# Group convolution on one Trainium2 core: from twelve accumulating products per step to four 32-column tiles fed from rows gathered through DRAM

## The chip, the cores and the metric

One core of a Trainium2 chip runs the whole program. The number reported is the time of one execution on the device in microseconds (us); lower is better. Three executions were timed (median 732.78 us, from 731.9 to 734.84), and one more was profiled.

## What is computed

The input `x` is 128 samples of 32 rows by 512 columns. In short, for each sample:

```
a  = mixing(x, cond)                  # 32x32 row mix per sample, weights from a small network on cond
x1 = x + attention(a) @ Wo            # 32 query heads of 16, 8 key/value heads, causal over the 32 rows
z  = conv1d(x1, weight)               # 9 taps along the 512 columns, pad 4; 4 groups of 8 channels in, 8 out
     + cond @ c_weight.T + bias       #   (a channel is one of the 32 rows)
out = x1 + z @ base_W.T + base_b + lora(z)   # lora: 8 experts of rank 16, weighted by a router
router: softmax(z @ router_W.T + router_b) over 15, the 8 largest kept
```

Products that need full precision use a split of each float32 value into a high and a low part (three matmuls: high*high, high*low, low*high); the convolution, the mixing and the transposes use plain float32.

## The kernel before, in words

**Tiling.** Four samples (128 rows) form a group; there are 32 groups. The 512 columns are kept as 4 phases of 128 (column 4n+j is phase j, index n). The work of a group is spread over four steps of a software pipeline: `iterate` calls every engine's `steps(t)` for t from -1 to 34, of which t = 4 to 30 run as a hardware loop and the rest are written out. In step t the engines do the queries, keys, scores, softmax and values of group t, the mixing of group t+1, the output projection (`project`) and the convolution of group t-1, the feed-forward product of group t-2 and the last (lora) part of group t-3.

**Order.** Each engine has its own list, written out by hand, and waits on semaphores. There is no scheduler. TensorE in step t (lines 605 to 652): `queries`, `keys_values`, `lora`, `project`, `transpose_qk`, `mix`, `scores`, `feed_forward`, `transpose_p`, `values`, `conv`, `transpose_hw`, `transpose_o`. A helper `product` (line 377) issues the split matmuls of `queries`, `keys_values` and `project`.

**The convolution** (lines 552 to 560): for each of 4 samples and each of 3 shifts one float32 matmul, 128 x 128 into 128 columns, with the input itself as the stationary operand. So the input must lie with (phase, channel) on the partitions. `by_phase` (line 280) makes that layout, `x1ph`, out of `x1` with 16 copies of 32 x 128: 8 on ScalarE (its copies are recorded at line 665) and 8 on VectorE (line 284). Output rows come out as the pixels, so that `zs` (after the addition at line 1031 of `convb`, a bias that was broadcast to 2 MB in the prologue) is split into `z_hi` (ScalarE) and `z_lo` (GpSimd, line 808) and used as stationary operand of `feed_forward` straight away.

**feed_forward** (lines 524 to 534): 12 terms, each one matmul into bank 6 (384 columns) and one into bank 7 (272 columns: the last phase of the base product, and the lora and router columns), in turn. `ar_ps` is raised at the end. ScalarE then copies `arS`; VectorE does `route`, ScalarE `ex`, VectorE `route2`, which ends with `hw` (line 971); TensorE needs that in `transpose_hw` (line 585), before `transpose_o` (line 591), which itself needs `normalize` (lines 1018, 1020).

**SyncE's queue** in a step (lines 346 to 357): load `xr` once `x1` is written, store `out` once it is there, load the next `xm` once `mix` is done.

**Prologue.** Tap weights are transposed and masked to `convW`; `ctxb` and `convb` are built; in step 0 TensorE waits for the loaded mixing weights (`mixw_in2`) and mixes before `scores(0)`, and runs 8 extra products after `prepare_ar` (`keep_warm`, line 430).

## Time and profile before

| what | value |
|---|---|
| timed executions, median (lowest to highest) | 732.78 us (731.9 to 734.84) |
| profiled execution, its own time | 736.14 us |
| its span in the profile | 733.8 us |
| TensorE matmul busy | 696.9 us, 95% of the span |
| VectorE busy | 528.8 us, 72% |
| ScalarE busy | 262.8 us, 36% |
| GpSimd busy | 149.5 us, 20% |
| instructions | 13835 |
| DMA | 35.45 MB, 48 GB/s over the span |
| mean granted TensorE clock | 0.99 |

The span runs from the first to the last instruction; the execution's own time has 2.3 us more around it. A float32 matmul is recorded as two loads and two matmuls, so the 12 matmuls of the convolution stand as 24. Durations of matmuls overlap by pipelining; the distance from one start to the next is what a matmul costs in a stream. A line "engine line op out<-in xN" merges N instructions in a row.

### The profile page before, as it was taken

The numbers are of one execution on the slowest core, as the hardware profiler recorded it, in microseconds if no ns is written. First come the engines' busy times: TensorE is split into PE (matmuls) and PEld (weight loads), VectorE is DVE, ScalarE is ACT, GpSimd is POOL, SyncE is SP. The second block draws the span as 40 slices with busy tenths as digits, with TensorE's granted clock in tenths as the row PEclk, the third lists the DMA queues.
The fourth block names the chain that finished last, engine by engine and source line by source line (L and its number), as shares of the span: only waits on it lengthen the run. The fifth ranks groups of instructions, "written<-read, shape, count | busy, mean of one in ns | idle before, by whom it ended". The sixth has DMA issues, their size and how long they took to land.

```text
span 733.8 us, 13835 instructions
## 1 busy us (share of the span) xinstructions
PE 696.9 (95%) x4850; PEld 623.2 (85%) x4882; DVE 528.8 (72%) x1488; ACT 262.8 (36%) x635; POOL 149.5 (20%) x116
## 2 busy tenths in 40 slices
PE   6799999999999999999999999999999999999994
PEld 4578989888988988898888888988888898888884
DVE  5557777777777777777787777777777777777763
ACT  4244443432344343333433332344333234433330
POOL 6222111122112121221212122121212212121211
PEclk9999999999999999999999999999999999999997
DMA  7870011110011111100111110011111001110100
GB/s 175 167 269 29 30 44 44 43 43 24 21 41 43 43 43 43 34 23 29 43 43 43 43 43 14 29 43 43 43 43 43 14 29 43 43 43 29 29 15 29
DMA packets 27394, 35.45 MB, mean 48 GB/s; under 512 B 11651, under 2 KB 13347, under 8 KB 26998
## 3 DMA queue, kind: packets, MB, share of 16 engines
q1 hardware_dynamic: 26374, 34.87, 16.0%
q0 software_dynamic: 144, 0.28, 0.2%
q10 hardware_dynamic: 864, 0.14, 0.1%
q8 instruction: 7, 0.11, 0.1%
q14 instruction: 5, 0.04, 0.0%
HBM read 26.35 MB, written 8.93 MB: 48 GB/s over the span
## 4 chain that ended last, share of the span: by engine, by line
PE 89%; ACT 3%; SPq 3%; issue 2%; DVE 2%; DMA 1%; DVEq 0%
PE ps L377 31%; PE ps L558 12%; PE ps L532 10%; PE ps L577 8%; PE ps L533 6%; PE ps L547 5%; PE ps L473 4%; PE ps L507 3%; ACT raw L665 3%; PE ps L565 2%; PE ps L591 2%; PE ps L521 2%; PE ps L543 2%; SPq L308 1%; DMA mixw_dram<-convb 1%
## 5 line engine op out<-in xcount | busy, mean ns | idle before, releaser
L665 ACT ACTIVATE qk_t<-ps 128x512 f32<-128x512 f32 x32 | 19.1, 597 | 226.8 <-PE ps L522 226.8
L822 POOL TENSOR_TENSOR y_lo<-ys,y_hi 128x512 fp32r<-128x512 f32 x31 | 39.4, 1271 | 267.4 <-ACT y_hi L665 267.4
L665 ACT ACTIVATE x1ph<-raw 32x128 f32<-32x128 f32 x256 | 79.0, 309 | 40.8 <-DVE raw L1063 38.2
L558 PE MATMUL ps<-convW,x1ph 128*128 128x128 f32 x768 | 92.6, 277 | 0.4 <-ACT x1ph L665 0.4
L377 PE MATMUL ps<-wqkv_hi,y_hi 128*128 128x512 f32 (+1 forms) x256 | 90.8, 355 | 0.4
L558 PEld LDWEIGHTS ps<-convW,x1ph 128*128 128x128 f32 x768 | 88.3, 192 | 0.7 <-ACT x1ph L665 0.7
L377 PE MATMUL ps<-wqkv_hi,y_lo 128*128 128x512 f32 (+1 forms) x256 | 87.5, 342 | 0.0
L377 PE MATMUL ps<-wqkv_lo,y_hi 128*128 128x512 f32 (+1 forms) x256 | 87.5, 342 | 0.0
L816 POOL TENSOR_TENSOR raw<-raw,basebB 128x512 f32<-128x512 f32 x32 | 49.3, 1540 | 143.5 <-DVE raw L1055 143.5
L577 PEld LDWEIGHTS ps<-vm,raw 128*128 128x128 f32 x512 | 59.6, 191 | 15.9 <-ACT raw L665 13.2
L577 PE MATMUL ps<-vm,raw 128*128 128x68 f32 x512 | 63.9, 278 | 8.4 <-ACT raw L665 8.4
L808 POOL TENSOR_TENSOR z_lo<-raw,z_hi 128x512 fp32r<-128x512 f32 x32 | 41.2, 1288 | 145.7 <-ACT z_hi L665 145.7
L981 DVE TENSOR_TENSOR network<-ps,cst 128x512 f32<-128x512 f32 x64 | 31.5, 491 | 53.2 <-PE ps L377 51.8
L1009 DVE TENSOR_REDUCE mx<-ps 128x16 f32<-128x512 f32 x64 | 43.9, 686 | 31.3 <-PE ps L547 31.3
L377 PEld LDWEIGHTS ps<-wqkv_hi,y_hi 128*128 128x128 f32 x256 | 48.9, 191 | 12.5 <-issue 5.6
L284 DVE COPY x1ph<-raw 32x128 f32<-32x128 f32 x256 | 55.7, 217 | 3.0
L377 PEld LDWEIGHTS ps<-wqkv_lo,y_hi 128*128 128x128 f32 x256 | 49.1, 192 | 6.1
L377 PEld LDWEIGHTS ps<-wqkv_hi,y_lo 128*128 128x128 f32 x256 | 48.9, 191 | 6.0
L377 PE MATMUL ps<-wo_hi,oT_hi 128*128 128x512 f32 x128 | 51.7, 404 | 0.0
L377 PE MATMUL ps<-wo_lo,oT_hi 128*128 128x512 f32 x128 | 50.3, 393 | 0.0
L377 PE MATMUL ps<-wo_hi,oT_lo 128*128 128x512 f32 x128 | 50.3, 393 | 0.0
L1000 DVE TENSOR_TENSOR qk_t<-ps,cst 128x512 f32<-128x512 f32 x32 | 22.1, 691 | 36.9 <-PE ps L522 36.9
(176 smaller groups left out, 1523.0 us busy)
## 6 DMA issues: line engine op xcount, KB each, us to landing
xm<-x SPq DMA_DIRECT2D x32, 256.0 KB, 2.6
xr<-x SPq DMA_DIRECT2D x32, 256.0 KB, 2.8
out<-raw SPq DMA_DIRECT2D x32, 256.0 KB, 2.0
convb<-convb_dram SPq DMA_DIRECT2D x1, 2048.0 KB, 11.6
mixb<-mixb_dram SPq DMA_DIRECT2D x1, 1792.0 KB, 7.3
raw<-L_attn_Wq SPq DMA_DIRECT2D x4, 256.0 KB, 5.5
raw<-L_attn_Wo SPq DMA_DIRECT2D x8, 128.0 KB, 5.1
raw<-L_ffn_base_W SPq DMA_DIRECT2D x1, 1024.0 KB, 5.9
```

The source lines that it names most:

```text
L284: last = copy(x1ph[S * j:S * (j + 1), b, 1:P + 1], x1[S * b:S * (b + 1), j, :])
L377: last = mm(dst, a, b, start=(n == 0), stop=(n == 3 * len(left) - 1))
L532: mm(ps[:, 6, 0:BASE6], a[:, j, :], b[:, j, 0:BASE6], start=first, stop=False)
L533: last = mm(ps[:, 7, 0:P + NAR], a[:, j, :], b[:, j, BASE6:D + NAR], start=first, stop=final)
L547: last = mm(ps[:, h, b * P:(b + 1) * P], qT[rows, b, :, :].rearrange("p g q -> p (g q)"), kT[rows, b, :, :].rearrange("p k m -> p (k m)"), ...
L558: last = mm(zo[:, :, b * S:(b + 1) * S], x1ph[:, b, s:s + P], convW[:, s, :, :], start=(s == 0), stop=(s == SHIFTS - 1))
L577: last = mm(ps[:, 4 + k // 4, (k % 4) * NB * VW:(k % 4 + 1) * NB * VW], prT[:, k, :], vm[:, k, :, :].rearrange("p b c -> p (b c)"), start= ...
L665: return nc.scalar.activation(dst, src, ACT.Copy)
L808: nc.gpsimd.tensor_tensor(z_lo[:, :, :].rearrange("p j n -> p (j n)"), zs, z_hi[:, :, :].rearrange("p j n -> p (j n)").bitcast(F32), ALU.s ...
L816: nc.gpsimd.tensor_tensor(x1b, x1, basebB[:, :].rearrange("p (n j) -> p j n", j=PH), ALU.add).then_inc(x1b_sb, 1)
L822: nc.gpsimd.tensor_tensor(y_lo[:, :], ys[:, :], y_hi[:, :].bitcast(F32), ALU.subtract).then_inc(y_lo_sb, 1)
L1009: v.tensor_reduce(m, s3, AX.X, ALU.max).then_inc(mx_sb, 1)
```

## The change

Input to the convolution: `x1` now has a column of zeros on either side of each phase. It is stored to DRAM (`x1_dram`) in each step, then gathered back with three DMAs, one per shift, into `xc`: 96 partitions (shift, 8 channels of a group, 4 phases) by 16 (sample, group) by 128. Each group of channels is one float32 matmul, 96 rows, 32 stationary columns, 512 moving columns, whose result goes to partitions 32g to 32g+31 of bank 1. The tap weights are the stationary operand now. The result has (channel, phase) on the partitions; the bias is per partition (`biasT`), and four transposes turn it back (`transpose_z`, after `transpose_qk` of the next step) into bank 7, from which `z_hi` and `z_lo` are made; `z_lo` goes from GpSimd to VectorE. `feed_forward` issues the 12 matmuls into bank 7 first, then the 12 into bank 6. `transpose_hw` goes ahead of `conv`. On VectorE the `x1` addition goes ahead of `keys`, `route` behind `softmax`, `route2` ahead of `normalize`. GpSimd makes `x1c` (x1 plus bias) and copies it to `x1b` in the next step. The prologue loses `ctxb`, `convb` and its 2 MB load, and the 8 extra products of step 0; there `mix(1)` and its wait come after `scores(0)` and `prepare_conv`.

```diff
...
     for t in range(G - 1, G + 3):
         steps(t)
-def by_phase(copy, phases):
-
-    for j in phases:
-        for b in range(NB):
-            last = copy(x1ph[S * j:S * (j + 1), b, 1:P + 1], x1[S * b:S * (b + 1), j, :])
-    return last
+def z_transposed():
+
+    return ps[:, 7, :].rearrange("p (q j o) -> p j q o", j=PH, o=CG)
 block = ctx.enter_context(nc.Block())
...
 load_mixw(1, 4, mixw_in2)
 sp.dma_start(rawbase, baseW.rearrange("(p j) l -> p j l", j=PH)).then_inc(ld["base"], 16)
 sp.dma_start(mixw_dram[4 * NB:B, :, :], aggS[4 * NB:B, :, :]).then_inc(mixw_out, 16)
-sp.wait_ge(ctx_sb, 1)
-sp.dma_start(convb_dram, ctxb[:, :]).then_inc(ctx_dram, 16)
 sp.wait_ge(mixw_out, 16)
 load_mixw(4, G, mixw_in)
 sp.dma_start(mixb[:, 4 * P:], mixb_row[4 * P:].partition_broadcast(P)).then_inc(mixb_in2, 16)
-sp.wait_ge(ctx_dram, 16)
-sp.wait_ge(mixw0_sb, 1)
-sp.wait_ge(mixb0_ps, 1)
-sp.dma_start(convb[:, :], convb_dram.rearrange("b s -> (b s)").partition_broadcast(P)).then_inc(convb_in, 16)
 def steps(t):
-    if live(t - 1):
-        wait(sp, x1_sb, t - 1)
-        sp.dma_start(xr[:, :], group(x_g, t - 1)).then_inc(xr_in, 16)
     if live(t - 3):
         wait(sp, out_sb, t - 2)
         sp.dma_start(group(out_g, t - 3), outS).then_inc(out_st, 16)
+    if live(t - 1):
+        sp.wait_ge(x1_sb, t)
+        sp.dma_start(x1_dram.rearrange("q (i j) n -> (q i) j n", j=PH), x1p[:, :, :]).then_inc(x1_out, 16)
     if live(t + 1) and live(t + 2) and not peeled(t, -1):
         wait(sp, y_ps, t + 2)
         sp.dma_start(xm[:, :], group(x_g, t + 2)).then_inc(xm_in, 16)
+
+    if live(t):
+
+        wait(sp, z_ps, t - 1)
+        sp.dma_start(xr[:, :], group(x_g, t)).then_inc(xr_in, 16)
+    if live(t - 1):
+        if not live(t):
+            wait(sp, z_ps, t - 1)
+        sp.wait_ge(x1_out, 16 * t)
+        for s in range(SHIFTS):
+            sp.dma_start(xc[S * s:S * (s + 1), :, :],
+                         x1_dram[:, :, s:s + P].rearrange("q r n -> r q n")).then_inc(xc_in, 16)
 for t in range(-1, 4):
     steps(t)
...
         if j % 2:
             last.then_inc(arT_ps, 1)
+def prepare_conv():
+
+    pe.wait_ge(cvR_sb, 1)
+    for j in range(PH):
+        nc.tensor.transpose(ps[0:SHIFTS * S, 4, j * S:(j + 1) * S],
+                            cvR[:, j, :, :, :].rearrange("o s i a -> o (s i a)"),
+                            cst[0:S, C_ID:C_ID + S])
+    pe.wait_ge(fsideR_sb, 1)
+    pe.wait_ge(ones_sb, 1)
+    mm(ps[:, 4, P:P + B], ccT[:, :, :, :].rearrange("p g j o -> p (g j o)"), condT[:, :], start=True, stop=False)
+    mm(ps[:, 4, P:P + B], fsideR[:, :, :, :].rearrange("p g j o -> p (g j o)"), ones8[0:1, :], start=False, stop=True
+       ).then_inc(cv_ps, 1)
+
 def prepare_lora():
     pe.wait_ge(ld["B"], 16 * PH)
...
     pe.wait_ge(z_hi_sb, u + 1)
     pe.wait_ge(z_lo_sb, u + 1)
     wait(pe, out_sb, u)
-    for j in range(PH):
-        for n, (a, b) in enumerate(((z_hi, ffn_hi), (z_hi, ffn_lo), (z_lo, ffn_hi))):
-            first, final = j == 0 and n == 0, j == PH - 1 and n == 2
-            mm(ps[:, 6, 0:BASE6], a[:, j, :], b[:, j, 0:BASE6], start=first, stop=False)
-            last = mm(ps[:, 7, 0:P + NAR], a[:, j, :], b[:, j, BASE6:D + NAR], start=first, stop=final)
+    terms = [(a[:, j, :], b[:, j, :]) for j in range(PH)
+             for a, b in ((z_hi, ffn_hi), (z_hi, ffn_lo), (z_lo, ffn_hi))]
+    for n, (a, b) in enumerate(terms):
+        last = mm(ps[:, 7, 0:P + NAR], a, b[:, BASE6:D + NAR], start=(n == 0), stop=(n == len(terms) - 1))
     last.then_inc(ar_ps, 1)
+    for n, (a, b) in enumerate(terms):
+        mm(ps[:, 6, 0:BASE6], a, b[:, 0:BASE6], start=(n == 0), stop=False)
 def scores(t):
     pe.wait_ge(qT_sb, t + 1)
...
                 last.then_inc(s_ps, 1)
 def conv(u):
-    pe.wait_ge(ph_act, u + 1)
-    pe.wait_ge(ph_dve, u + 1)
-    zo = ps[:, 1, :].rearrange("p (j t) -> p j t", j=PH)
+    pe.wait_ge(xc_in, 16 * SHIFTS * (u + 1))
+    for g in range(S // CG):
+        last = mm(ps[S * g:S * (g + 1), 1, :], convW[:, g, :, :].rearrange("p j o -> p (j o)"),
+                  xc.rearrange("p (b g) n -> p g b n", g=S // CG)[:, g, :, :],
+                  start=True, stop=True)
+    last.then_inc(z_ps, 1)
+
+def transpose_z(u):
+    pe.wait_ge(zs_sb, u + 1)
     for b in range(NB):
-        for s in range(SHIFTS):
-            last = mm(zo[:, :, b * S:(b + 1) * S], x1ph[:, b, s:s + P],
-                      convW[:, s, :, :], start=(s == 0), stop=(s == SHIFTS - 1))
-    last.then_inc(z_ps, 1)
+        last = nc.tensor.transpose(ps[:, 7, b * P:(b + 1) * P], zs[:, b * P:(b + 1) * P], ident)
+    last.then_inc(zT_ps, 1)
 def transpose_p(t):
     pe.wait_ge(p_sb, 2 * (t + 1))
...
 if live(t):
     transpose_qk(t)
+if live(t - 2):
+    transpose_z(t - 2)
 if peeled(t, 1):
     pe.wait_ge(prep_sb, 1)
     prepare_base((0, 1))
 if peeled(t, -1):
     pe.wait_ge(mixw0_sb, 1)
-if peeled(t, 0):
-    pe.wait_ge(mixw_in2, 16 * NB)
 if peeled(t, 2):
     pe.wait_ge(mixw_in, 16 * NB)
-if live(t + 1):
+if live(t + 1) and not peeled(t, 0):
     mix(t + 1)
 if peeled(t, -1):
     mixing_weights()
...
 if peeled(t, 0):
     prepare_ar()
-    pe.wait_ge(cv_sb, 1)
-    keep_warm(8)
+    prepare_conv()
+    pe.wait_ge(mixw_in2, 16 * NB)
+    mix(t + 1)
 if peeled(t, 1):
     prepare_base((2, 3))
     pe.wait_ge(x1_sb, 1)
...
 if live(t):
     transpose_p(t)
+if peeled(t, 0):
+    pe.wait_ge(convW_sb, 1)
 if live(t):
     values(t)
+if live(t - 2):
+    transpose_hw(t - 2)
 if live(t - 1):
     conv(t - 1)
-if live(t - 2):
-    transpose_hw(t - 2)
 if live(t):
     transpose_o(t)
...
 if live(t):
     act.wait_ge(qT_ps, t + 1)
     copy(qT, ps[:, 2, :].rearrange("p (g b q) -> p b g q", g=NQ, b=NB)).then_inc(qT_sb, 1)
+if live(t - 2):
+    act.wait_ge(zT_ps, t - 1)
+    copy(z_hi[:, :, :].rearrange("p j (q o) -> p j q o", o=CG), z_transposed()).then_inc(z_hi_sb, 1)
 if peeled(t, 1):
     prepare_base((0, 1))
-if live(t - 1):
-    act.wait_ge(x1_sb, t)
-    by_phase(copy, (1, 3)).then_inc(ph_act, 1)
-if live(t):
-    for h in range(2):
+for h in range(2):
+    if live(t):
         act.wait_ge(sx_sb, 2 * t + 1 + h)
         nc.scalar.activation(pr.rearrange("p (h k b m) -> p h b k m", h=2, k=HK, b=NB)[:, h, :, :, :],
                              sx.rearrange("p (h b k m) -> p h b k m", h=2, b=NB, k=HK)[:, h, :, :, :],
                              ACT.Exp, scale=HD ** -0.5).then_inc(p_sb, 1)
+    if h == 0 and live(t - 2):
+        act.wait_ge(ar_ps, t - 1)
+        copy(arS[:, :], ps[:, 7, P:P + NAR]).then_inc(ar_sb, 1)
+if live(t - 2):
+    act.wait_ge(lgs_sb, t - 1)
+    nc.scalar.activation(ex[:, :], lgs[:, :], ACT.Exp).then_inc(ex_sb, 1)
+if live(t):
     for h in range(2):
         act.wait_ge(pT_ps, 2 * t + 1 + h)
         copy(prT[:, 4 * h:4 * h + 4, :].rearrange("p k n -> p (k n)"), ps[:, 2 + h, :]).then_inc(pT_sb, 1)
-if live(t - 2):
-    act.wait_ge(ar_ps, t - 1)
-    copy(arS[:, :], ps[:, 7, P:P + NAR]).then_inc(ar_sb, 1)
 if live(t + 1):
     act.wait_ge(ys_sb, t + 2)
     copy(y_hi[:, :], ys[:, :]).then_inc(y_hi_sb, 1)
...
 def steps(t):
     if live(t - 2):
-        pool.wait_ge(zs_sb, t - 1)
-        pool.wait_ge(z_hi_sb, t - 1)
-        nc.gpsimd.tensor_tensor(z_lo[:, :, :].rearrange("p j n -> p (j n)"), zs,
-                                z_hi[:, :, :].rearrange("p j n -> p (j n)").bitcast(F32),
-                                ALU.subtract).then_inc(z_lo_sb, 1)
-    if live(t - 2):
-        pool.wait_ge(x1_sb, t - 1)
+
+        wait(pool, out_sb, t - 2)
+        pool.wait_ge(x1c_sb, t - 1)
+        if peeled(t, 2):
+            pool.wait_ge(pads_sb, 1)
+        nc.gpsimd.tensor_tensor(x1b, x1c, zero[:, :].unsqueeze(2).broadcast_to([P, PH, P]), ALU.add).then_inc(x1b_sb, 1)
+    if live(t - 1):
+        pool.wait_ge(x1_sb, t)
         pool.wait_ge(ld["basebB"], 16)
-
-        wait(pool, out_sb, t - 2)
-        nc.gpsimd.tensor_tensor(x1b, x1, basebB[:, :].rearrange("p (n j) -> p j n", j=PH),
-                                ALU.add).then_inc(x1b_sb, 1)
+        wait(pool, x1b_sb, t - 1)
+        nc.gpsimd.tensor_tensor(x1c, x1, basebB[:, :].rearrange("p (n j) -> p j n", j=PH),
+                                ALU.add).then_inc(x1c_sb, 1)
     if peeled(t, 0):
         prepare_wo((0, 1))
     if live(t + 1) and not peeled(t, -1):
...
 def steps(t):
     if peeled(t, 2):
-        dve.wait_ge(convb_in, 16)
         dve.wait_ge(baseT_ps, PH)
     if live(t - 2):
         dve.wait_ge(z_ps, t - 1)
-        v.tensor_tensor(zs.rearrange("p (j n) -> p j n", j=PH), ps[:, 1, :].rearrange("p (j n) -> p j n", j=PH),
-                        convb[:, bass.ds((t - 2) * P, P)].unsqueeze(1).broadcast_to([P, PH, P]),
+        v.tensor_tensor(zs.rearrange("p (b n) -> p b n", b=NB), ps[:, 1, :].rearrange("p (b n) -> p b n", b=NB),
+                        biasT[:, bass.ds((t - 2) * NB, NB)].unsqueeze(2).broadcast_to([P, NB, P]),
                         ALU.add).then_inc(zs_sb, 1)
     if live(t - 3):
         dve.wait_ge(hwT_hi_sb, t - 2)
...
     out3 = outS.rearrange("p (n j) -> p j n", j=PH)
     v.tensor_tensor(out3[:, 0:3, :], ps[:, 6, 0:BASE6].rearrange("p (j n) -> p j n", j=3), x1b[:, 0:3, :], ALU.add)
     v.tensor_tensor(out3[:, 3, :], ps[:, 5, 0:P], x1b[:, 3, :], ALU.add).then_inc(out_sb, 1)
-if live(t):
-    keys(t)
 if live(t - 1):
     dve.wait_ge(wo_ps, t)
     dve.wait_ge(xr_in, 16 * t)
-    wait(dve, x1b_sb, t - 1)
+    wait(dve, x1c_sb, t - 1)
+    wait(dve, x1_out, 16 * (t - 1))
     v.tensor_tensor(x1, ps[:, 4, :].rearrange("p (j n) -> p j n", j=PH),
                     xr[:, :].rearrange("p (n j) -> p j n", j=PH), ALU.add).then_inc(x1_sb, 1)
+if live(t):
+    keys(t)
+if live(t - 2):
+    dve.wait_ge(z_hi_sb, t - 1)
+    minus(z_lo[:, :, :].rearrange("p j (q o) -> p j q o", o=CG), z_transposed(),
+          z_hi[:, :, :].rearrange("p j (q o) -> p j q o", o=CG)).then_inc(z_lo_sb, 1)
 if peeled(t, 1):
     prepare_base((0, 1))
 if live(t):
     softmax(t)
+if live(t - 2):
+    route(t - 2)
 if peeled(t, -1):
     prepare_q(0)
     dve.wait_ge(mixb0_sb, 1)
...
```

## Rows read from the trace of the kernel before

**Rows 1.** The profile's page: TensorE's busy time; the chain by engine, by line.
```profile
PE 696.9 (95%) x4850; PEld 623.2 (85%) x4882; DVE 528.8 (72%) x1488; ACT 262.8 (36%) x635; POOL 149.5 (20%) x116
...
PE 89%; ACT 3%; SPq 3%; issue 2%; DVE 2%; DMA 1%; DVEq 0%
PE ps L377 31%; PE ps L558 12%; PE ps L532 10%; PE ps L577 8%; PE ps L533 6%; PE ps L547 5%; PE ps L473 4%; PE ps L507 3%; ACT raw L665 3%; PE ps L565 2%; PE ps L591 2%; PE ps L521 2%; PE ps L543 2%; SPq L308 1%; DMA mixw_dram<-convb 1%
```
**Rows 2.** Busy time by engine in one stretch; then clock, DMA share, GB/s.
```profile
319.00:340.30 21.30, 20.90 (x151) 18.88 (x151) 15.94 (x46) 7.73 (x19) 4.10 (x3) 1.00 0.10 37
```
**Rows 3.** The chain in order of time: queries of steps 4 and 31.
```profile
108.00 4.17 PE ps L377 x24
...
683.16 4.17 PE ps L377 x24
```
**Rows 4.** The page's costliest groups: the convolution and what feeds it.
```profile
L665 ACT ACTIVATE x1ph<-raw 32x128 f32<-32x128 f32 x256 | 79.0, 309 | 40.8 <-DVE raw L1063 38.2
L558 PE MATMUL ps<-convW,x1ph 128*128 128x128 f32 x768 | 92.6, 277 | 0.4 <-ACT x1ph L665 0.4
...
L284 DVE COPY x1ph<-raw 32x128 f32<-32x128 f32 x256 | 55.7, 217 | 3.0
```
**Rows 5.** TensorE in one step of the loop, in order of time.
```profile
330.59 0.38 PE L543 MATMUL ps<-causal,ident 128*128 128x512 bf16 x1
330.90 1.16 PE L547 MATMUL ps<-qk_t 64*128 64x128 f32 x16
331.99 0.44 PE L532 MATMUL ps<-ffn_hi,z_hi 128*128 128x384 f32 x1
...
335.69 1.04 PE L565 MATMUL ps<-cst,raw 128*128 128x128 f32 x8
336.98 2.00 PE L577 MATMUL ps<-vm,raw 128*128 128x68 f32 x16 [0.25 <-ACT raw L665]
338.82 2.89 PE L558 MATMUL ps<-convW,x1ph 128*128 128x128 f32 x24
341.55 0.28 PE L585 MATMUL ps<-cst,hw 128*128 128x128 f32 x1
341.67 0.60 PE L591 MATMUL ps<-cst,raw 128*128 128x128 f32 x4
```
**Rows 6.** TensorE in the prologue, in order of time.
```profile
14.10 2.08 PE L473 MATMUL ps<-mixw,xm 128*128 128x128 f32 x8
16.11 3.78 PE L424 MATMUL ps<-convb,attT 8*128 8x512 f32 x4
```
**Rows 7.** VectorE in the same step as rows 5.
```profile
330.19 1.05 DVE L1063 TENSOR_TENSOR raw<-ps,xr 128x512 f32<-128x512 f32 x1
332.09 0.69 DVE L1009 TENSOR_REDUCE mx<-ps 128x16 f32<-128x512 f32 x1 [0.85 <-PE ps L547]
...
339.31 0.42 DVE L1020 TENSOR_TENSOR raw<-ps,rz 128x256 f32<-128x256 f32 x1
```
**Rows 8.** DMA issues: KB each, median us from issue to landing.
```profile
xr<-x SPq DMA_DIRECT2D x32, 256.0 KB, 2.8
out<-raw SPq DMA_DIRECT2D x32, 256.0 KB, 2.0
...
raw<-L_attn_Wv SPq DMA_DIRECT2D x1, 256.0 KB, 7.0
```
**Rows 9.** Busy time by engine while the weights load; last number GB/s.
```profile
10.00:15.00 5.00, 3.23 (x15) 2.45 (x15) 3.51 (x12) 2.79 (x8) 3.22 (x6) 1.00 1.16 257
```
**Rows 10.** Waits: TensorE's `mix(1)`, for the mixing weights.
```profile
PE ps L473 <- DMA mixw<-mixw_dram: 2.2, 1, 2.2
```
**Rows 11.** The last steps: TensorE and ScalarE, in order of time.
```profile
712.91 2.94 PE L558 MATMUL ps<-convW,x1ph 128*128 128x128 f32 x24 [0.44 <-ACT x1ph L665]
...
724.81 0.29 ACT L665 ACTIVATE arS<-ps 128x144 f32<-128x144 f32 x1 [7.56 <-PE ps L533]
...
727.93 0.33 PE L585 MATMUL ps<-cst,hw 128*128 128x128 f32 x1 [3.16 <-DVE hw L971]
```

126 lines of the change are left out of this document (56 added, 70 removed).

## The prediction, made before the changed kernel was run

> **What bounds the kernel now.** I read the busy times first: TensorE is at it for 696.9 of 733.8 us, and the chain that ended last is 89% TensorE, of which line 558, the convolution, is 12% [rows 1]. Then one stretch in the middle: of 21.30 us TensorE works 20.90 at the full clock, VectorE 15.94, ScalarE 7.73, GpSimd 4.10, and the DMA engines are a tenth used [rows 2]. Then the chain in order of time: the queries of step 4 start at 108.00 and those of step 31 at 683.16, so a step takes 575.16 / 27 = 21.30 us [rows 3]. So the loop is TensorE's list, played without gaps (the only one of note is 0.25 us ahead of the values [rows 5]). What shortens that list counts 32 times; what is taken off ScalarE or VectorE counts only if TensorE waits for it.
>
> **The convolution now.** Its 24 records stand from 338.82 to the next one at 341.55: 2.73 us, 0.114 each [rows 5]. All 768 take 92.6 us by their busy time [rows 4]. Taken away: 2.73 per step. With it go the 16 layout copies: 79.0 us on ScalarE and 55.7 on VectorE over the run [rows 4], 2.5 and 1.7 a step. Both engines have idle time, so I cost that at nothing; its worth is slack.
>
> **The four tiles.** Each new matmul streams 512 columns where an old one streams 128. What does a plain float32 record of 512 columns take? The prologue has four, at half the pace: 3.78 / 4 = 0.95, right behind 128-column ones of 2.08 / 8 = 0.26 [rows 6]; a quarter of the one is 0.24, so time goes with columns, and at full pace a record is 4 x 0.114 = 0.455. There are 8 of them (two per matmul). In series that is 3.64, worse than now. If the four tiles run side by side it is two slots, 0.91. Those are the two ends. The nearest row is the scores' (line 547), which use 64 rows of the array each: 16 records begin at 330.90 and feed_forward follows at 331.99, 1.09 for what would be 1.82 in series and 0.91 in 8 slots of two [rows 5]. So parts of the array do work side by side, with 0.18 around them. I take full overlap and 0.2 for going in and out: 1.11 per step.
>
> The Trainium skill, TensorE: Matmul & The Clock Gate, Part 3, says that weight loads overlap with running matmuls only where their row groups differ, and here all four tiles use the same rows. By that rule the loads would stand in the open. No row here shows a 32-column load; as an estimate, a quarter of a 128-column record is 0.03, eight of them 0.23 per step, and the forecast would be 7 us higher. It lies inside my range, and I don't take it, since the same part measures column tiles as nearly as quick as row tiles.
>
> **Transposing back.** Four more transposes; the eight of line 565 take 1.04 with their tail, and four of line 591 0.60 where each start is 0.11 from the last [rows 5]: 0.45 per step. The two orders of feed_forward hold the same 24 matmuls, 3.70 us from 331.99 to 335.69: nothing.
>
> Sum per step: -2.73 + 1.11 + 0.45 = -1.17, and 32 groups: -37.4.
>
> **What could now be late, step by step** (times of the step in rows 5 and 7, all moved 0.45 later by the transposes where TensorE sets them).
> *The scores* need kT. The x1 addition came behind keys and ended at 331.24 [rows 7]; with the two swapped, kT is there at 331.24 if nothing starts sooner, and x1 at 330.55 (keys is a pass of the size of line 1009's, 0.69 [rows 7]). The scores' first product would start at 330.59 + 0.45 = 331.04 [rows 5]: at most 0.2 lost.
> *z_lo* is one more such pass on VectorE, till 331.9 (z_hi, on ScalarE, runs beside keys); feed_forward starts at 332.44 [rows 5]. Covered by 0.5.
> *The probabilities*: softmax [rows 7] starts 0.45 later, like feed_forward's end; the arS copy of 0.3 [rows 11] goes between the two exponentials, which are two VectorE passes apart. Nothing.
> *The router chain*: from the arS copy to hw's transpose it is 727.93 - 724.81 = 3.1 us when nothing is in its way [rows 11]. Bank 7 is now done halfway, near 334.2, but VectorE takes it up after softmax (332.54 and four passes of 0.69: 335.3) and puts ys in between: 335.3 + 3.1 - 0.3 + 0.7 = 338.8, and transpose_hw comes at 341.55 - 2.73 + 0.45 = 339.3 [rows 5]. Covered by 0.5.
> *transpose_o* waits for normalize, whose last multiply ended at 339.73, 0.91 after the convolution had started [rows 5, 7]. Before, 2.73 us of convolution covered that; now transpose_hw (0.11) and 1.11. Cover by 0.3, and less if route2, now ahead of normalize on VectorE, is late: from 339.0 two halves of some 0.65 end at 340.3, and transpose_o is due at 340.5. The thinnest place; each 0.1 lost there costs 3.2 us.
> *SyncE's queue*: out, then the x1 store, xm (behind mix), xr, then it waits for the x1 store and issues three gathers. Behind that wait stands only the next step's out store. *GpSimd* does 3 passes as before, 4.1 us of 20.
>
> **The round trip.** x1 is written by 330.6. The out store of the same size lands in 2.0, a load in 2.8 [rows 8]; the x1 rows come in smaller pieces, so landed 2.4 to 3.2 later: 333.0 to 333.8. The gathers move 3 x 256 KB; in the prologue, with pieces of 512 bytes and less among them, 257 GB/s were moved [rows 9]: 3.1 us, and some 1.5 of latency (2.8 less what 256 KB take at that rate): 337.6 to 338.4. The convolution would want it at 339.4. So it is hidden, with 1.0 to 1.8 us to spare. The other end is a load of 512-byte pieces that landed in 7.0 us in a crowded queue [rows 8].
>
> **Prologue and end.** Step 0 waited 2.2 us for the mixing weights with the scores behind it [rows 10]; now the scores cover that; the 8 extra products go, about as much conv preparation comes, and values(0) waits for convW. I take -1.5 (0 to -4). At the end conv(31) began 0.44 after its layout copies [rows 11]; now a store and gathers, 2.4 + 4.6 = 7 us by the figures above, stand in a stretch with 3.7 us of feed_forward: about +3. Against it the router chain of the last group, 3.1, runs beside the base columns. I take 0 (-2 to +4).
>
> **Sum.** -37.4 - 1.5 + 0 = -38.9, plus 0.1 per step for small new waits (an estimate from the two places with 0.2 to 0.3 of cover), 3: -36. The profiled execution took 736.14, so it would be 700; it stood 3.4 above the median of the timed ones, and against 732.78 it is **697 us**.
>
> **Rivals.**
> *A, the tiles overlap only in part.* The Trainium skill, same page and part, says that matmuls start and end strictly in program order. A float32 matmul is two records on one tile, so the second of tile 0 must wait for its first, and tile 1 behind it. As a mechanism of this kernel: slots 0a | 0b 1a | 1b 2a | 2b 3a | 3b, five of 0.455 = 2.28, and the step is -2.73 + 2.48 + 0.45 = +0.20: +6.4 - 1.5, **738**. The scores' 1.09 us would fit 9 such slots (1.02) about as well as 8 (0.91), so the trace doesn't exclude it; for the forecast speaks that it needs 0.18 of switching in the one case and 0.07 in the other, and switching of almost nothing is less likely. Chance 0.10.
> *B, no overlap at all*: 3.64 + 0.2, +1.56 a step, **781**. Rows 5 speak against it for row tiles; column tiles aren't in the trace. 0.06.
> *C, slower by the gathers.* Place: TensorE's wait ahead of conv. If a gather takes the 7.0 us of rows 8 from its issue (333.4, and an estimated 0.8 for the two issues ahead), it lands at 341.2, 1.8 late each step: -36 + 58, **755**. It decides from 5.2 us of landing on; above 6.4 the kernel is slower than before. For it: 1536 small pieces, xm and xr in the same queue. Against it: the DMA engines are a tenth busy [rows 2], and the 7.0 was queued behind six other loads. 0.10, half of it light.
> *D, it does less than it says*: the convolution shrinks, but TensorE then waits for normalize or kT, half a microsecond each step: **713**. 0.06.
> Forecast: 0.68.
>
> **Chances and range.** A measurement of this kernel tells 0.5%, 3.7 us, from no change. Faster: 0.68 + D 0.06 + light C 0.03 = 0.77. Same: parts of A and C, 0.05. Slower: 0.18. The forecast's own range is 684 (no new waits, prologue -4) to 710 (loads in the open, small waits doubled); to leave out no more than 2 in 10 it reaches over D and light C to 732.
>
> **What would show it.** Right: a step of 20.1 to 20.3 us; eight conv records in about 1.1 us, starting in fours; waits ahead of conv for the gather near zero; conv's chain share about 5%; ScalarE and VectorE down by some 70 and 35 us. Wrong: conv records 0.45 apart (B) or starting in pairs (A); TensorE waiting on a DMA into xc, or a landing time over 5 us (C); an idle ahead of line-591 transposes on normalize, or ahead of the scores (D).

## The result, and the profile after

The changed kernel takes **709.45 us** (median of 4 executions, 704.92 to 711.31), the kernel before beside it 733.22 (4 executions, 731.9 to 734.84): ratio 0.965, 95% interval 0.962 to 0.968, a gain of 24 us where 36 were forecast. The profiled executions are 709.07 and 736.14 us, 27.1 apart; the one of before stood about 3 above its median, the one of after at its own. The gain is clear of the spread; its size is two thirds of the forecast.

The profile's page of the changed kernel: busy times, the chain that ended last, and the time from issue to landing of the DMAs (the last number, in us). `scratch<-x_dram` are the gathers into `xc`.

```profile
PE 660.4 (93%) x4455; PEld 557.2 (79%) x4487; DVE 499.2 (71%) x1264; ACT 181.0 (26%) x379; POOL 141.3 (20%) x117
...
PE 86%; DMA 5%; ACT 3%; issue 3%; DVE 2%; SPq 1%; DVEq 0%; ACTq 0%
PE ps L381 33%; PE ps L543 9%; PE ps L590 8%; PE ps L540 7%; PE ps L564 5%; PE ps L556 4%; PE ps L481 4%; DMA scratch<-x_dram 4%; PE ps L515 3%; PE ps L604 3%; ACT raw L681 2%; PE ps L578 2%; PE ps L529 2%; PE ps L572 2%; PE ps L552 2%
...
scratch<-x_dram SPq DMA_DIRECT2D x96, 256.0 KB, 5.2
x_dram<-x1p SPq DMA_DIRECT2D x32, 260.0 KB, 2.0
xm<-x SPq DMA_DIRECT2D x32, 256.0 KB, 2.8
xr<-x SPq DMA_DIRECT2D x32, 256.0 KB, 2.9
```

Against [rows 1], TensorE has 36.5 us less work, the convolution fell from 12% of the chain to 5% (line 564), and ScalarE lost 82 us, VectorE 30. New in the chain is a DMA at 4%, of which more below. One step of the loop, as in [rows 2]:

```profile
299.00:319.30 20.30, 19.63 (x143) 16.77 (x142) 15.14 (x38) 5.14 (x11) 3.83 (x3) 1.00 0.35 90
```

The chain in order of time has the queries of the steps as in [rows 3]; the first and the last of 25 steps without a wait in them:

```profile
145.88 4.20 PE ps L381 x24
...
653.29 4.20 PE ps L381 x24
```

(653.29 - 145.88) / 25 = 20.30 us each, against 21.30; the 27 from step 4 to step 31 average 20.31. DMA share went from 0.10 to 0.35. TensorE in the stretch that changed, beside [rows 5]:

```profile
357.09 0.60 PE L572 MATMUL ps<-cst,raw 128*128 128x128 f32 x4
357.53 1.06 PE L481 MATMUL ps<-mixw,xm 128*128 x8
359.00 0.38 PE L552 MATMUL ps<-causal,ident 128*128 128x512 bf16 x1 [0.42 <-issue]
359.31 1.16 PE L556 MATMUL ps<-qk_t 64*128 64x128 f32 x16
...
367.27 0.28 PE L598 MATMUL ps<-cst,hw 128*128 128x128 f32 x1
367.48 1.07 PE L564 MATMUL ps<-scratch,convW 96*32 96x512 f32 x8
368.47 0.66 PE L604 MATMUL ps<-cst,raw 128*128 128x128 f32 x4
```

By starts, the convolution takes 368.47 - 367.48 = 0.99 us (2.73 before), `transpose_hw` ahead of it 0.21 (0.12 before), the transposes back 0.44, and 0.42 us of idle stand ahead of the scores. In the kernel before that idle was 0.15:

```profile
373.25 0.38 PE L543 MATMUL ps<-causal,ident 128*128 128x512 bf16 x1 [0.15 <-issue]
```

That is -2.73 + 0.99 + 0.09 + 0.44 + 0.27 = -0.94 of the measured -0.99. The rest lies in the stretches around it, as means over 25 steps: from `transpose_o` to the next queries 0.54 before and 0.40 after, against some 0.07 more in the projections and `feed_forward`.

**Where the 27 us came from** (spans 733.8 and 706.8; starts of the queries of each step):

| stretch | before | after | difference | forecast |
|---|---|---|---|---|
| to the start of step 1 | 43.4 | 41.3 | -2.1 | -1.5 |
| steps 1 to 3 | 64.4 | 63.3 | -1.1 | -3.2 |
| steps 4 to 30, 27 of them | 575.2 | 548.5 | -26.7 | -28.9 |
| queries of step 31 to the end | 50.8 | 53.7 | +2.9 | -2.1 |

(The forecast's column splits its -1.07 a step over the convolutions in each stretch: 3, 27 and 2.) The loop did nearly what was said; the edges kept the rest. But only the loop repeats: of the kernels below, e11 has the changed kernel's steps 1 to 3 and its end, and took 61.5 and 52.4 us for them where this execution took 63.3 and 53.7. So some 3 us of the edges are this execution's and not the kernel's.

### The profile page after: what moved, and what is told of

Same layout as the page of the kernel before. It is cut to its first block, busy times and chain, and to the rows that moved or that the text cites. A ratio compares the mean times of both kernels' runs of the same rounds, so it can differ in the third digit from the quotient of the medians.

```text
span 706.8 us, 12716 instructions
## 1 busy us (share of the span) xinstructions
PE 660.4 (93%) x4455; PEld 557.2 (79%) x4487; DVE 499.2 (71%) x1264; ACT 181.0 (26%) x379; POOL 141.3 (20%) x117
## 4 chain that ended last, share of the span: by engine, by line
PE 86%; DMA 5%; ACT 3%; issue 3%; DVE 2%; SPq 1%; DVEq 0%; ACTq 0%
PE ps L381 33%; PE ps L543 9%; PE ps L590 8%; PE ps L540 7%; PE ps L564 5%; PE ps L556 4%; PE ps L481 4%; DMA scratch<-x_dram 4%; PE ps L515 3%; PE ps L604 3%; ACT raw L681 2%; PE ps L578 2%; PE ps L529 2%; PE ps L572 2%; PE ps L552 2%
## 5 line engine op out<-in xcount | busy, mean ns | idle before, releaser
L826 POOL TENSOR_TENSOR raw<-raw,zero 128x512 f32<-128x512 f32 x32 | 33.2, 1038 | 281.0 <-DVE raw L1073 281.0
L681 ACT ACTIVATE qk_t<-ps 128x512 f32<-128x512 f32 x32 | 19.1, 597 | 238.8 <-PE ps L530 238.8
L756 ACT ACTIVATE raw<-raw 128x512 f32<-128x512 f32 x64 | 40.5, 632 | 130.1 <-DVE raw L1030 130.1
L831 POOL TENSOR_TENSOR raw<-x1p,basebB 128x512 f32<-128x512 f32 x32 | 49.0, 1531 | 47.4 <-DVE x1p L1080 47.4
L1080 DVE TENSOR_TENSOR x1p<-ps,xr 128x512 f32<-128x512 f32 x32 | 35.2, 1099 | 29.7 <-PE ps L381 29.7
L1030 DVE TENSOR_TENSOR raw<-ps,mx 128x512 f32<-128x512 f32 x64 | 44.3, 692 | 2.2
L543 PE MATMUL ps<-ffn_hi,z_lo 128*128 128x384 f32 x128 | 43.9, 343 | 0.0
L543 PE MATMUL ps<-ffn_lo,z_hi 128*128 128x384 f32 x128 | 43.8, 342 | 0.0
```

The costliest lines, as they stand in the source:

```text
L543: mm(ps[:, 6, 0:BASE6], a, b[:, 0:BASE6], start=(n == 0), stop=False)
L681: return nc.scalar.activation(dst, src, ACT.Copy)
L756: nc.scalar.activation(pr.rearrange("p (h k b m) -> p h b k m", h=2, k=HK, b=NB)[:, h, :, :, :], sx.rearrange("p (h b k m) -> p h b k m", ...
L831: nc.gpsimd.tensor_tensor(x1c, x1, basebB[:, :].rearrange("p (n j) -> p j n", j=PH), ALU.add).then_inc(x1c_sb, 1)
L1030: v.tensor_tensor(sx[:, D * h:D * h + D].rearrange("p (h m) -> p h m", m=S), s3, m.unsqueeze(2).broadcast_to([P, 16, S]), ALU.subtract).th ...
L1080: v.tensor_tensor(x1, ps[:, 4, :].rearrange("p (j n) -> p j n", j=PH), xr[:, :].rearrange("p (n j) -> p j n", j=PH), ALU.add).then_inc(x1_ ...
```

## The experiments

Twelve kernels, each the changed kernel with one edit unless said otherwise; e10 and e12 were executed six and five times, the others once. A step is the mean from the queries of step 4 to those of step 31; it repeats within 0.02 us from one execution to the next (20.31, and 20.30 in four kernels that didn't change it). The total doesn't (last section), nor do the edges, so the step is what I compare.

### Is it the overlap of the four tiles?

**e1**: all four products write to partitions 0 to 31.

```diff
-    last = mm(ps[S * g:S * (g + 1), 1, :], convW[:, g, :, :].rearrange("p j o -> p (j o)"),
+    last = mm(ps[0:S, 1, :], convW[:, g, :, :].rearrange("p j o -> p (j o)"),
...
```

> The changed kernel with all four matmuls of the convolution sent to the same 32 columns of the array (partitions 0 to 31), one after another, so three quarters of z are stale; the same loads, streams, DMAs and order otherwise. Theory (the gain of the convolution is that four tiles run side by side): eight records 0.455 us apart, 3.64 instead of 0.91, 2.7 us more per step: a step of 23.0 us, some 795 us in all. Rival (the gain comes from fewer and longer instructions, or from the copies taken off ScalarE and VectorE, and the tiles matter little): below 720 us.

Measured: 786.0 us, step 22.86, +2.54.

```profile
357.36 3.62 PE L564 MATMUL ps<-scratch,convW 96*32 96x512 f32 x8
360.91 0.66 PE L604 MATMUL ps<-cst,raw 128*128 128x128 f32 x4
```

3.55 us from start to next start against 0.99: rival B's price nearly to the figure (3.64), and the whole gain is the overlap, 3.6 times. In the changed kernel's trace the first four matmul records of the convolution start within 0.02 us of each other and the other four 0.45 us later. The records don't say which tile they belong to, but on one tile, in e1, each starts 0.43 to 0.45 after the last, so four that start together must be on four tiles. Two slots of four: rival A, five slots, isn't what happens.

### Do the transposes back cost their 0.45?

**e2**: one of the four.

```diff
-    for b in range(NB):
+    for b in range(1):
         last = nc.tensor.transpose(ps[:, 7, b * P:(b + 1) * P], zs[:, b * P:(b + 1) * P], ident)
```

> The changed kernel with one of the four transposes of z instead of four; the rest of z is stale. Theory (the loop is TensorE's list played without gaps): three transposes of 0.11 less, a step of 19.97 instead of 20.30, 10 us less in all. Rival (a gather from DRAM ends last ahead of the convolution, with 0.4 us to spare or none): the step shrinks by 0.1 or less, since the x1 addition, the store and the gathers start from the projection, which stands ahead of the transposes.

Measured: 709.85 us, step 20.30, unchanged. Three transposes fewer, and the idle ahead of the scores grew from 0.42 to 0.74, by what they took:

```profile
359.87 0.27 PE L572 MATMUL ps<-cst,raw 128*128 128x128 f32 x1
...
361.77 0.38 PE L552 MATMUL ps<-causal,ident 128*128 128x512 bf16 x1 [0.74 <-issue]
```

The theory "TensorE's list has no gap here" falls. The scores' start is set elsewhere; VectorE at the same time in the changed kernel shows by what:

```profile
356.99 1.09 DVE L1080 TENSOR_TENSOR x1p<-ps,xr 128x512 f32<-128x512 f32 x1 [0.93 <-PE ps L381]
358.01 0.68 DVE L1019 TENSOR_TENSOR qk_t<-ps,cst 128x512 f32<-128x512 f32 x1
```

The keys (line 1019) come behind the `x1` addition and end at 358.69, and the scores begin 0.31 later. That distance is 0.32 us in every one of 25 steps, in this kernel, in e2 and in the kernel before alike. The timeline calls the idle "issue", but in step 0, where TensorE waits longer, the same distance stands between the two (29.14 to 29.45), and there it names the keys (`qk_t`); e7 tests it:

```profile
29.45 0.38 PE L552 MATMUL ps<-causal,ident 128*128 128x512 bf16 x1 [1.05 <-DVE qk_t L1019]
```

### Did the layout copies matter?

**e3**: the kernel *before*, with 2 of its 16 copies (1 on each engine).

```diff
-            for j in phases:
-                for b in range(NB):
+            for j in phases[:1]:
+                for b in range(samples):
```

(`samples` is 1.)

> The kernel before with 2 of its 16 layout copies (one on ScalarE, one on VectorE), so the convolution reads stale input; TensorE's list is unchanged. Theory (copies on ScalarE and VectorE were hidden behind TensorE and their removal is worth nothing in the loop): a step of 21.2 to 21.3 us as before, at most 3 us less in all (the last convolution no longer waits 0.44 us). Rival (part of the gain of the change comes from relieving ScalarE and VectorE): 10 us or more less.

Measured: 732.93 us beside 734.69, step 21.29 beside 21.30. Taking away 14 copies, some 120 us of engine time over the run, is worth nothing by itself, as costed.

### Is "router columns first" needed?

**e4**: `feed_forward` in the order of before, bank 6 and bank 7 in turn, all else as changed.

```diff
     for n, (a, b) in enumerate(terms):
+        mm(ps[:, 6, 0:BASE6], a, b[:, 0:BASE6], start=(n == 0), stop=False)
         last = mm(ps[:, 7, 0:P + NAR], a, b[:, BASE6:D + NAR], start=(n == 0), stop=(n == len(terms) - 1))
     last.then_inc(ar_ps, 1)
-    for n, (a, b) in enumerate(terms):
-        mm(ps[:, 6, 0:BASE6], a, b[:, 0:BASE6], start=(n == 0), stop=False)
```

> The changed kernel with feed_forward's 24 matmuls in the order of the kernel before (bank 6 and bank 7 in turn), so that the router columns are complete 1.9 us later. Theory (the halves are issued apart because ScalarE and VectorE now have route and the arS copy ahead of work that TensorE waits for): ScalarE stands at arS while the second exponential is ready, the transposes of the probabilities start 0.5 to 1.3 us late, and normalize is late behind route2: a step of 20.9 to 21.9 us instead of 20.30, 20 to 45 us more in all. Rival (the order is only for the last group, where the chain of the router stands alone): a step of 20.30 and 2 to 3 us more at the end.

Measured: 743.0 us beside 732.77, step 21.37, +1.06. ScalarE in one step and TensorE in the one before, in order of time (lines 681, 756 and 578 of the changed kernel stand one higher here):

```profile
377.25 0.29 ACT L680 ACTIVATE arS<-ps 128x144 f32<-128x144 f32 x1 [1.71 <-PE ps L541]
```

```profile
356.74 1.09 PE L577 MATMUL ps<-cst,raw 128*128 128x128 f32 x8 [0.90 <-ACT raw L755]
```

ScalarE holds the second exponential back behind the `arS` copy, which waits for the last of `feed_forward`; the probabilities come 0.9 us late. So "router columns first" is no extra. Without it, and with the engines' other new orders as they are, the whole gain is lost: the step is that of the kernel before (21.37 against 21.30), and of the 10 us above it 8 are the end (58.6 us from the queries of step 31 on, against 50.8).

### The gathers: hidden in the loop, bare at the end

**e5**: one gather instead of three in all steps but the first; it waits for that one.

```diff
-    for s in range(SHIFTS):
+    for s in range(SHIFTS if peeled(t, 1) else 1):
...
-    pe.wait_ge(xc_in, 16 * SHIFTS * (u + 1))
+    pe.wait_ge(xc_in, 16 * (u + SHIFTS))
```

> The changed kernel with one gather of three from the second group on (two thirds of the gathered rows are stale from the first group). Theory (the gathers are hidden in the loop and exposed at both ends): a step of 20.30 us as before, the wait ahead of the last convolution (2.5 us) shrinks to about 1 and the clock falls for less long at the end: 2 to 6 us less in all. Rival (the gather is what ends last in every step): a step shorter by 0.1 us or more.

Measured: 704.62 us, step 20.30, unchanged; the end from step 31 on 49.6 us against 53.7. In the loop, then, the gathers cost nothing. SyncE in the changed kernel:

```profile
317.52 0.34 SPq L346 DMA_DIRECT2D x_dram<-x1p  x1
318.24 0.34 SPq L349 DMA_DIRECT2D xm<-x  x1
318.84 0.34 SPq L354 DMA_DIRECT2D xr<-x  x1
319.58 1.39 SPq L360 DMA_DIRECT2D scratch<-x_dram  x3
```

and its waits on the gathers (in all, times, the longest):

```profile
PEld ps L564 <- DMA scratch<-x_dram: 4.4, 4, 2.7
```

Four waits in 32 steps, all near the two ends. But the margin is thin. In the step of these rows the last of the three gathers lands at 326.01 and the convolution starts at 326.88. Over 25 steps the rows are there 0.3 to 1.1 us ahead of it, 0.5 at the median. (The page's 5.2 us is the median of all 96 gathers; the third of each step takes 5.3 to 6.1 us, 5.9 at the median.)

**e6**: gathers issued ahead of `xm` and `xr` on SyncE. The queue's wait on the last convolution (`z_ps`) goes, since the wait on `x1` behind that convolution implies it.

> The changed kernel with the three gathers ahead of the loads of xm and xr in SyncE's queue, without the wait on the last convolution that the order of the others implies. Theory (gathers hidden in the loop, competing with 512 KB of other loads): they land about 1 us sooner, the step stays at 20.30 us because nothing waits for them. Rival (the 0.1 us ahead of the convolution is a wait for the gather): step 20.2.

Measured: 705.5 us, step 20.30. The page:

```profile
scratch<-x_dram SPq DMA_DIRECT2D x96, 256.0 KB, 4.3
...
xm<-x SPq DMA_DIRECT2D x32, 256.0 KB, 4.9
xr<-x SPq DMA_DIRECT2D x32, 256.0 KB, 5.0
```

The gathers land 0.9 us sooner by their median, the two loads behind them 2.1 later, and neither moves the step: nothing in the loop waits for either. The rows are now there 1.0 to 1.5 us ahead of the convolution.

**e7**: on VectorE, `keys` ahead of the `x1` addition again. **e8**: this and e6's order together.

```diff
+    if live(t):
+        keys(t)
     if live(t - 1):
         dve.wait_ge(wo_ps, t)
...
-    if live(t):
-        keys(t)
```

> The changed kernel with keys ahead of the x1 addition on VectorE, as before the change. Theory (what holds TensorE in the loop is kT, late by 0.3 us at the scores, which is why leaving out three transposes gained nothing): the idle ahead of the scores falls from 0.42 to about 0.1, but x1 is 0.7 later and with it store and gathers, which have 0.4 us to spare: 0.3 gained at the scores less 0.6 lost ahead of the convolution, a step of 20.4 to 20.7 us. Rival (the gathers have more to spare than 0.4): a step of 20.0.

> Keys ahead of the x1 addition, and the gathers ahead of xm and xr. Theory: both waits are gone, a step of 20.0 us, some 8 us less in all than the changed kernel. Rival (store and gathers from the later x1 still end last): 20.2 or more, with a DMA wait ahead of the convolution.

Measured: e7 717.55 us, step 20.69, slower; e8 694.83 us, step 19.98. In e7 the idle ahead of the scores is gone, as the reading of e2 has it, but another has come:

```profile
363.74 1.06 PE L481 MATMUL ps<-mixw,xm 128*128 x8
364.85 0.38 PE L552 MATMUL ps<-causal,ident 128*128 128x512 bf16 x1
...
373.11 0.28 PE L598 MATMUL ps<-cst,hw 128*128 128x128 f32 x1
373.81 1.06 PE L564 MATMUL ps<-scratch,convW 96*32 96x512 f32 x8 [0.42 <-DMA scratch<-x_dram]
```

```profile
PEld ps L564 <- DMA scratch<-x_dram: 26.8, 31, 2.3
```

Counted from the step's first query, `x1` is written 0.9 us later and the whole round trip with it, while the scores and all behind them come 0.4 sooner. A margin of 0.5 can't pay for both, and nearly every step waits now, 0.2 to 1.1 us each, 0.6 on average. In e8 the sooner landing pays. TensorE in e8:

```profile
369.41 1.06 PE L477 MATMUL ps<-mixw,xm 128*128 x8
370.51 0.38 PE L548 MATMUL ps<-causal,ident 128*128 128x512 bf16 x1
```

No idle ahead of the scores, and none ahead of the convolution in this part of the loop either (its eight records begin at 359.05, 0.21 behind `transpose_hw`). But it is just in time: the last gather lands at 359.01. Over the whole run e8's weight loads wait for a gather in 13 steps:

```profile
PEld ps L560 <- DMA scratch<-x_dram: 6.1, 13, 2.2
```

Within the loop TensorE loses at most 0.2 us by it in a step, so the gather is the next bound, with nothing to spare. So the changed kernel's two orders (the addition first, the loads first) are each one half of a pair: turned back alone the one is neutral and the other a loss, both together are worth 0.32 us a step, 9 over the loop. e8's total, 15 under the changed kernel's, has a quick start in it (last section). And e7 is rival C in small: the gather does become the bound once it starts 0.9 later.

### The end

The changed kernel's last steps: TensorE in order of time, and a window of the last 23 us:

```profile
687.65 1.94 PE L564 MATMUL ps<-scratch,convW 96*32 96x512 f32 x8 [2.51 <-DMA scratch<-x_dram]
...
694.83 0.57 PE L540 MATMUL ps<-ffn_hi,z_hi 128*128 128x272 f32 x1 [1.46 <-DVE z_lo L850]
```

```profile
684.00:707.00 23.00, 12.54 (x50) 9.64 (x50) 7.30 (x25) 1.66 (x5) 1.04 (x1) 0.70 0.16 44
```

2.5 us for the gather, and behind it a convolution of 1.94 instead of 1.07 and `feed_forward` at 0.23 from one start to the next instead of 0.125: the granted clock of this stretch (the last number but two of the window's row) is 0.70, so much of it ran at 1.2 GHz, not 2.4. **e9**: 10 products whose result nobody reads, ahead of the last convolution, in the time in which TensorE waits for the gather.

```diff
+    if peeled(t, G):
+        pe.wait_ge(x1_sb, G)
+        keep_warm(10)
     if live(t - 1):
         conv(t - 1)
```

> The changed kernel with ten extra 512-column bf16 products into a free bank in step 32, between transpose_hw and the last convolution, where TensorE waits 2.5 us for the gather. Theory (the end of the changed kernel lost 3 to 4 us because TensorE stood still there and then worked at 1.2 GHz: the last convolution took 1.94 instead of 1.07 and feed_forward's first 19 matmuls twice their time): the clock stays up after the wait, from the queries of step 31 to the end 53.7 us become 49 to 51. Rival (the end is set by the chain of transfers and copies, not by the clock): 53 or more.

Measured: 708.99 us; from step 31 to the end 49.95 instead of 53.73.

```profile
688.91 2.11 PE L425 MATMUL ps<-causal,ident 128*128 128x512 bf16 x9
690.95 1.06 PE L564 MATMUL ps<-scratch,convW 96*32 96x512 f32 x8
```

```profile
684.00:707.00 23.00, 13.60 (x82) 10.18 (x82) 8.83 (x34) 2.16 (x7) 1.48 (x2) 0.94 0.24 65
```

The clock of the same stretch is 0.94, the convolution back at 1.06, and the end 3.8 us shorter. Not all of that is the clock: here the last convolution starts 34.2 us behind the queries of step 31, 0.4 sooner than in the changed kernel's execution. And e11, whose end is the changed kernel's too, needed 52.4 us. From the start of the last convolution on it is 15.75 us here, 19.1 in the changed kernel and 18.5 in e11, so the products are worth some 3 us. The total hides it: step 1 of this execution started at 46.4, 5 us later than in the changed kernel's (41.3).

### The start

**e11**: `mix(1)` ahead of `scores(0)`, as before the change.

```diff
+    if peeled(t, 0):
+        pe.wait_ge(mixw_in2, 16 * NB)
-    if live(t + 1) and not peeled(t, 0):
+    if live(t + 1):
         mix(t + 1)
...
-    pe.wait_ge(mixw_in2, 16 * NB)
-    mix(t + 1)
```

> The changed kernel with mix(1) and its wait for the mixing weights ahead of scores(0) again, as before the change. Theory (the order of step 0 is worth the wait of 2.2 us that it hides): the queries of step 1 start at 43 to 44 us instead of 40 to 41.5, the loop as it was (20.30). Rival (the start of step 1 is set by the chain of normalize and projection weights, or by the clock): 40 to 42.

Measured: 707.27 us, step 1 at 43.0, the lower edge of what the theory gives. Inconclusive: kernels with one and the same step 0 started step 1 anywhere from 40.1 to 46.4.

### All together

**e10**: e8 and e9 in one.

> Keys ahead of the x1 addition, gathers ahead of xm and xr, and the ten extra products of the last step, together. Theory: the parts add up: a step of 19.98 as in the kernel with the first two, an end 3 us shorter: 691 to 693 us, a ratio to the kernel before of 0.942 to 0.947. Rival (the one look at the first two was a lucky prologue): 697 or more, 0.950 or more.

Measured: median **697.03 us** (6 executions, 694.48 to 701.36) against 735.65 of the kernel before (11 executions, 732.73 to 739.55): ratio 0.947, interval 0.944 to 0.950, against 0.965 (0.962 to 0.968) of the change: some 12 us faster than the changed kernel. The ratio is at the theory's upper edge; the median is not the theory's 691 to 693 but where the rival begins, and with executions from 694.5 to 701.4 these runs don't tell the two apart. The step is 20.02, so the loop's part is there. The end took 51.1 us in the profiled execution, not e9's 50.0, and 1.8 less than e8's where 3 were said. Its last convolution ran at full pace, but the `feed_forward` behind it fell back to half pace, 0.23 us from one start to the next for its first 12 matmuls.

**e12**: e10 with ten more such products in step 0, 6 behind the keys and values and 4 behind `transpose_qk`, where TensorE is idle.

```diff
+    if peeled(t, 0):
+        keep_warm(6)
...
     transpose_qk(t)
+    if peeled(t, 0):
+        keep_warm(4)
```

> The kernel of e10_all plus 10 extra bf16 products in step 0, placed where TensorE is idle: 6 behind the keys and values (idle 1.5 us in the changed kernel's profile, 2.8 in e10_all's) and 4 behind transpose_qk (idle 1.05 to 1.2). Their results are overwritten. Theory (the start of step 1, 40.1 to 46.4 us over the runs so far, is set by whether TensorE is granted its half clock after these idles): the scores of step 0 run at full pace (1.1 us, not 2.1), step 1 starts at 40 to 41.5 us, the executions lie within some 3 us of each other, and the median is 692 to 694 against 697.03 of e10_all. Rival 1 (the clock of the start hangs on something else): step 1 starts anywhere between 41 and 47 us, the spread stays at 7 us, the median at 696 to 698. Rival 2 (the products are themselves in the way of the transposes, 0.1 to 0.5 us each place, and the clock falls later, in the wait for the normalized values): step 1 at 42 to 44 us, median 695.

Measured: 697.04 us, the same median, but 5 executions within 1.8 us (695.76 to 697.59) where e10's lay within 6.9. Step 1 started at 42.9. TensorE in step 0 of e10, then of e12:

```profile
28.81 1.12 PE L525 MATMUL ps<-cst,qk 128*128 128x128 f32 x4 [2.77 <-DVE qk L1009]
...
31.91 2.08 PE L552 MATMUL ps<-qk_t 64*128 64x128 f32 x16
```

```profile
25.95 1.47 PE L421 MATMUL ps<-causal,ident 128*128 128x512 bf16 x6
...
30.65 1.16 PE L552 MATMUL ps<-qk_t 64*128 64x128 f32 x16
...
34.91 2.08 PE L477 MATMUL ps<-mixw,xm 128*128 128x128 f32 x8
```

The scores are back at full pace as the theory has it, but the mixing behind them is at half pace now; the start of step 1 is where rival 2 has it (42 to 44), though rival 1 allows it too. The median is rival 1's (696 to 698), 2 above rival 2's and 3 above the theory's. What the products may buy is the narrower spread of the theory, which five executions suggest and don't prove; the median is not improved.

## Why the prediction was right, and where it was off

709.45 lies in the range (684 to 732), at the upper end of the forecast's own (684 to 710), and the mechanism is the forecast's: the tiles overlap and the loop gets that much shorter. The size was 12 us off, and half of rival D's mechanism came true: TensorE does wait for kT in every step, 0.42 us against 0.15 before. The total is nearer to D's 713 than to 697, but mostly by other terms, as follows.

- **The convolution**: 1.11 with switching forecast, 0.99 + 0.09 = 1.08 measured; serial price 3.64 forecast, 3.55 in e1. The transfer from the scores' 64-row products to 32-column tiles held. Rivals A and B are out. The Trainium skill (TensorE: Matmul & The Clock Gate, Part 3) says weight loads overlap with running matmuls only where row groups differ, which would have put eight loads in the open. The trace doesn't bear that out for tiles of the same rows: all eight loads stand within 0.16 us, the last four of them begin when the first four matmuls have begun and end 0.3 us ahead of the next four, and the 0.99 us leave 0.08 beside two slots of 0.45, where the eight loads were estimated at 0.23.

```profile
347.18 0.16 PEld L564 LDWEIGHTS ps<-scratch,convW 96*32 96x32 f32 x8
```

  The other rule of the Trainium skill, same page and part, matmuls strictly in program order, gives rival A's five slots only if the two records of a product follow each other; the records stand in two slots, so either they don't or the rule doesn't hold here. No run tells which.
- **The transposes**: 0.44 measured against 0.45 forecast, yet e2 shows that three of them are free. The step that failed is the cover of the scores: "at most 0.2 lost" was to be a bound, and the sum carried 0.1 for all small waits together; 0.27 more than before was lost every step. The keys even ended 0.2 sooner than the bound allows. What it left out is the 0.32 from the end of the keys to the first product, and that the scores waited for the keys already: the row of 330.59 hides an idle of 0.15 us, at the limit below which the timeline marks none, so the list was not quite without gaps. The transposes' 0.44 and this 0.27 are one thing: the keys pass, behind the addition, sets the scores' start whatever TensorE does before. Over the 27 steps 0.17 beyond what was carried is 4.6 us; the stretch from the convolution to the next queries came some 0.1 a step cheaper than forecast, which leaves the loop's 2.
- **Normalize** kept the cover that was forecast, 0.3: the last multiply ended 0.28 ahead of `transpose_o` and nothing was lost. It was thin, but the scores were the thinnest place. Router chain, probabilities and `z_lo` were covered, as said. e4 shows how much the probabilities hang on the new order.
- **The gathers**: cover of 1.0 to 1.8 forecast, 0.5 measured. From `x1` to the last landing the sum had 7.0 to 7.8 us, and it took 8.9 (median of 25 steps). The store was sized too long (2.4 to 3.2, measured 2.0), the gathers too short: 3.1 + 1.5 = 4.6 against 6.8 from the store's landing to the last gather's. (By its own figures the 1.5 should have been 1.8.) In e6, ahead of `xm` and `xr`, it is 8.1 from `x1`, so 0.8 of it is the queue. Rival C was to decide from 5.2 us of landing on. The third gather took 5.9, and the wait still didn't come in the loop, since the convolution comes 9.4 behind `x1` and not 8.8 (the idle ahead of the scores is part of that). That is cover by luck: e7, which starts the round trip 0.9 later, shows C in force at +0.39 a step.
- **The end**: forecast 0 with +3 for the gathers and -3 for the router chain. The wait was 2.5 us (1.8 in e11), somewhat less than sized, and the router chain's wait went, as said. What the sum left out is the clock: after the idle ahead of the last convolution much of the rest ran at half pace, worth some 3 us (e9). With one gather (e5) the end is 4.1 shorter than the changed kernel's and 2.7 shorter than e11's, so either cure takes nearly all of it.
- **Steps 1 to 3**: -1.1 where -3.2 was forecast; by e9 and e11, whose steps 1 to 3 are the same program, -2.6 and -2.9. So most of this miss is the one execution. Its step 1 took 22.85 us, 0.7 of it a wait for the first gather:

```profile
61.69 1.77 PE L564 MATMUL ps<-scratch,convW 96*32 96x512 f32 x8 [0.70 <-DMA scratch<-x_dram]
```

  and part of the rest ran at reduced clock (0.68 from 40 to 44 us, 0.89 to 48, 0.72 from 60 to 66); in e8, with the full clock granted from 25 to 62 us, step 1 took 20.5. Start-up was costed by its instructions alone.
- **The base**: 3.4 us were taken off for the profiled execution of before; after's stood at its median. So 3 of the 12 us are that, 2 the loop, 7 the edges (5.0 at the end, 2.1 in steps 1 to 3, less 0.6 of the start), and of these 7 some 3 are the clock that this execution happened to get.

## What to carry to other kernels

When a product uses a quarter of the array's columns, give four of them their own column tiles and issue them back to back: here that is 3.6 times (e1), and it pays for a round trip through DRAM and for transposes back. The gain is only as good as the reorderings around it: e4 lost all of it to one order of issue, and e8 found 0.32 us a step in two swaps that are each worth nothing or less alone, so when one waiting place has just become thin, try the swaps that shift slack to it in pairs. When you check whether one engine covers for another, count the time from the end of a pass to the start of what needs it, 0.3 us here from the keys to the scores. And look at the two ends of a pipeline for idle stretches of TensorE that are followed by half clock; cost them in clock as well as in time.
